# Output projection applied to keys' values before the attention product, with reordered gate, division and row-factor steps

## The reference

```python
def _L0_xattn_ref(x, mask, k_cache, v_cache, wq, wk, wv, wo):      # k_cache = v_cache = ctx
    q, k_new, v_new = x @ wq.T, x @ wk.T, x @ wv.T
    k = concatenate([k_cache, k_new], axis=1); v = concatenate([v_cache, v_new], axis=1)
    attn = softmax(q @ k.T / 16)                                    # 64 queries x 128 keys
    return (attn @ v) @ wo.T
x = x + tanh(g_xattn[0]) * _L0_xattn_ref(_layernorm(x), mask, ctx, ctx, wq, wk, wv, wo)
x = x + tanh(g_ffn[0])   * _L0_ffn_ref(_layernorm(x), w1, w3, w2)       # gated, ternary weights, hidden 682
x = x + tanh(g_xattn[1]) * _L1_xattn_ref(64, 64, 256, w, u, _layernorm(x), ctx)   # recurrence (WKV)
x = x + tanh(g_ffn[1])   * _L1_ffn_ref(_layernorm(x), ...)              # shared expert + top 2 of 8 experts
```

## Time and profile before

| | |
|---|---|
| median of 3 runs | 781.95 us (781.42 to 788.72) |
| profiled execution | 784.78 us, span of the core 783.1 us |
| busy in the span | TensorE 728.9 us, VectorE 519.7, ScalarE 353.2, GpSimd 336.2 |
| turn 0 / turn 1 / one of turns 2 to 7 / the rest | 76.2 / 72.7 / 87.4 / 109.9 us |

### The profile page before, as it was taken

The page is one execution under the profiler, slowest core; times in us unless marked ns, Lnnn a source line. Parts: engine busy times, 40 slices in busy tenths (PEclk is TensorE's granted clock), DMA queues, the critical chain, the costliest instruction groups (busy, mean ns, idle before and its releaser), DMA issues. The chain is left out here.

```text
span 783.1 us, 13120 instructions
## 1 busy us (share of the span) xinstructions
PE 728.9 (93%) x4636; PEld 624.8 (80%) x4636; DVE 519.7 (66%) x926; ACT 353.2 (45%) x676; POOL 336.2 (43%) x345
## 2 busy tenths in 40 slices
PE   6978897799999999999999999999999999897996
PEld 6876696689887888789877888789877888786785
DVE  2766467773877478773877488764877478798432
ACT  3436513564356424654356434654365434623231
POOL 2024221381545435371545345362546345275254
PEclk8999999999999999999999999999999999999899
DMA  9170002010032001220032002120022010021111
GB/s 249 64 207 9 1 1 54 28 56 28 28 82 65 32 28 53 68 64 17 27 80 68 27 27 80 42 67 13 27 80 68 27 38 29 12 58 41 55 60 49
DMA packets 36212, 41.25 MB, mean 53 GB/s; under 512 B 3198, under 2 KB 27476, under 8 KB 36180
## 3 DMA queue, kind: packets, MB, share of 16 engines
q1 hardware_dynamic: 36180, 40.83, 17.9%
HBM read 36.49 MB, written 4.33 MB: 52 GB/s over the span
## 5 line engine op out<-in xcount | busy, mean ns | idle before, releaser
L1133 POOL TENSOR_TENSOR hid_l<-act_sb,hid_h 128x512 fp32r<-128x512 f32 x120 | 162.3, 1353 | 207.9 <-ACT hid_h L938 207.6
L1381 DVE SCALAR_TENSOR_TENSOR act_sb<-act_sb,gate_ps 128x512 f32<-128x512 f32 (+1 forms) x128 | 86.8, 678 | 112.2 <-ACT act_sb L920 112.0
L1142 POOL TENSOR_TENSOR act_sb<-act_sb,late 128x512 f32<-128x512 f32 x64 | 94.2, 1472 | 73.2 <-DVE act_sb L1383 70.0
L938 ACT ACTIVATE hid_h<-act_sb 128x512 fp32r<-128x512 f32 (+1 forms) x128 | 80.4, 628 | 98.1 <-POOL act_sb L1142 62.5
L482 PE MATMUL sums<-down_h,hid_h 128*128 128x256 f32 x320 | 92.3, 288 | 5.0 <-POOL hid_l L1133 5.0
L482 PE MATMUL sums<-down_h,hid_l 128*128 128x256 f32 x320 | 90.5, 283 | 0.0
L482 PE MATMUL sums<-down_l,hid_h 128*128 128x256 f32 x320 | 90.5, 283 | 0.0
L920 ACT ACTIVATE act_sb<-gate_ps 128x512 f32<-128x512 f32 x80 | 47.3, 591 | 84.0 <-PE up_ps L482 81.1
L1383 DVE TENSOR_TENSOR act_sb<-act_sb,up_ps 128x512 f32<-128x512 f32 x120 | 82.4, 687 | 4.1
L482 PEld LDWEIGHTS sums<-down_h,hid_h 128*128 128x128 f32 x320 | 61.1, 191 | 9.5 <-issue 7.1
L482 PE MATMUL gate_ps<-zm_h,gate_h 128*128 128x512 f32 x140 | 60.9, 435 | 8.1 <-DVE act_sb L1383 8.1
(11 more groups left out here) (197 smaller groups left out, 1689.8 us busy)
## 6 DMA issues: line engine op xcount, KB each, us to landing
late<-combine_rows SPq DMA_DIRECT2D x64, 256.0 KB, 3.1
ctx_tok<-in_ctx SPq DMA_DIRECT2D x8, 512.0 KB, 5.2
vals<-in_ctx SPq DMA_DIRECT2D x16, 256.0 KB, 5.7
out_x<-late SPq DMA_DIRECT2D x8, 512.0 KB, 3.1
xa<-in_x SPq DMA_DIRECT2D x7, 512.0 KB, 3.5
wk<-in_L_ffn_w SPq DMA_DIRECT2D x2, 682.0 KB
late<-in_L_ffn_w_down SPq DMA_DIRECT2D x1, 1024.0 KB, 7.3
wk<-in_L_ffn_w_gate SPq DMA_DIRECT2D x2, 512.0 KB, 4.8
```

The costliest lines, as they stand in the source:

```text
L938: nc.scalar.activation(hid_h[0:n, pos], act_sb[0:n, pos], ACT.Copy).then_inc(hid_h_set, 1)
L1133: nc.gpsimd.tensor_tensor(hid_l[:, pos], act_sb[:, pos], hid_h[:, pos].bitcast(F32), ALU.subtract).then_inc(hid_l_set, 1)
L1142: nc.gpsimd.tensor_tensor(act_sb[:, pos], act_sb[:, pos], comb_sb[:, pos], ALU.mult).then_inc(weighted, 1)
L1381: nc.vector.scalar_tensor_tensor(mine, mine, 1.0, gate_ps[pos][0:hidden_rows(chunk)], ALU.add, ALU.mult).then_inc(gated_one, 1)
```

## The change

Own value rows and context rows are multiplied by `wo` before the attention product. For the own rows that is done once for all, in turn 0: `turn_wv` and `fuse_wv_wo` replace the value weights by their product with `wo` (it stands in PSUM, and is split from there). For the context rows `context_out` multiplies the transposed context (already in `keys`) by `wo` in each turn, in two halves of the array (64 columns of weights each), and ScalarE copies the result into `vals`. `attend` then gives the projected rows directly, with weights of 64 columns from `probsT` and 256 moving columns from `vals`. `project`, the two copies to `qo` and the two context DMAs go; the load of `wo` moves ahead of the first context load. Around it: on VectorE `scan_values(1)` and both pieces of `divide(0)` move ahead of `row_max`, and `m_gate(6)` moves behind the second statistics; on ScalarE `normalise(A, 2)` moves ahead of `m_chunk(7)`; on GpSimd `row_factors(A, 2)` moves ahead of `m_weigh(6)`. The core of the diff:

```diff
 TRANSIT:  ... ("A","v0"), ("A","v1"), +("A","u0"), +("A","u1"), ("A","scores"), ("A","pT"), -("A","oT0"), -("A","oT1"), ("A","wo0") ...
@@ sync
+                sp.dma_start(wo[:], ...)                 # at the end of attention_weights, before ctx_row
-                    sp.dma_start(vals[S:P, :, 0], ctx_seqs[t.i, 0]).then_inc(ctx_val_in, 16)
-                    sp.dma_start(vals[0:S, :, 1], ctx_seqs[t.i, 1]).then_inc(ctx_val_in, 16)
@@ tensor
+            def turn_wv():
+                pe.wait_ge(qkv_in[2], 16)
+                for m in range(KH):
+                    for k in range(KH):
+                        last = nc.tensor.transpose(gate_ps[0][:, m * D + k * P:m * D + (k + 1) * P], raw_wv[:, k, m * P:(m + 1) * P], ident[:])
+                last.then_inc(fuse_turned, 1)
+            def fuse_wv_wo():
+                pe.wait_ge(fuse_kept, 1)
+                pe.wait_ge(wo_in, 16)
+                for k in range(KH):
+                    for m in range(KH):
+                        last = nc.tensor.matmul(up_ps[0][:, k * D:(k + 1) * D], wv_turned[:, m, k * P:(k + 1) * P], wo[:, m],
+                                                start=m == 0, stop=m == KH - 1)
+                last.then_inc(fuse_done, 1)
+            def context_out(t):
+                wait_taken(pe, t, "A", "ctxT0", "ctxT1", claims=("A", "u0"))
+                for pair in range(2):
+                    bank, full = claim(t, "A", f"u{pair}")
+                    for r in range(2):
+                        for k in range(KH):
+                            for q in range(2):
+                                last = nc.tensor.matmul(bank[(1 - q) * S:(2 - q) * S, r * D:(r + 1) * D], keys[:, k, 2 * pair + r, 1 + q],
+                                                        wo[:, k], start=k == 0, stop=k == KH - 1)
+                    last.then_inc(full, 1)
             def attend(t):
-                (16 products: weights vals[:, r, q, h * P:(h + 1) * P], moving probsT[:, cols], 64 columns)
-            def project(t): ... (8 products: weights qo, moving wo[:, k], 256 columns)
+                wait_taken(pe, t, "A", "v0", "v1", "u0", "u1", "pT", claims=("A", "wo0"))
+                        for q in range(2):
+                            tile = 2 * pair + r
+                            cols = slice((2 * tile + q) * S, (2 * tile + q + 1) * S)
+                            last = nc.tensor.matmul(bank[q * S:(q + 1) * S, r * D:(r + 1) * D], probsT[:, cols], vals[:, tile, q],
+                                                    start=True, stop=True)
@@ tensor, turn
                 if first:
                     keep_clock(12)
+                    turn_wv()
                 context_T(t)
 ...
-                    keep_clock(10)
+                    fuse_wv_wo()
+                    keep_clock(4)
                 z_T(t, "A", "z0T", za_row, 1)
 ...
                 values(t)
+                context_out(t)
                 m_down(3)
                 scores(t)
 ...
                 attend(t)
                 m_up(6)
-                if first:
-                    keep_clock(3)
-                project(t)
                 m_up(7)
@@ tensor, second:  context_T, keys_T, +context_out, scores, keep_clock(10), probs_T, keep_clock(3), attend, -keep_clock(3), -project
@@ scalar
-            def attend(t): ... (2 copies 128x512 to qo)
+            def keep_wv(): ... (wait fuse_turned, 1 copy 128x512)
+            def context_out(t): ... (per pair: 2 copies of 64x512 from the bank into vals)
@@ scalar, turn
-                    for name in ("wq", "wk", "wv"): high(name)
+                    high("wq"), high("wk"), keep_wv()
 ...
                 normalise(t, "A", 1, xa, za_row, rstd_a, shift_a)
+                if first:
+                    high("wv")
 ...
                 values(t)
+                context_out(t)
                 if first:
                     act.wait_ge(tern_in, 64)   # then the absolute sums, L981
 ...
                 m_chunk(6)
+                normalise(t, "A", 2, xa, za_row, rstd_a, shift_a)
                 m_chunk(7)
-                normalise(t, "A", 2, xa, za_row, rstd_a, shift_a)
@@ gpsimd, turn
                 m_low(5)
+                row_factors(t, "A", 2, ...)
                 m_weigh(6)
                 m_low(6)
-                row_factors(t, "A", 2, ...)
@@ vector, turn
                     add_to_values(t, 0)
+                    scan_values(t, 1)
+                    divide(t, 0, 0)
+                    divide(t, 0, 1)
                 row_max(t)
                 m_gate(5)
                 row_scale(t)
 ...
-                    scan_values(t, 1)
-                    divide(t, 0, 0)
-                m_gate(6)
-                if w:
-                    divide(t, 0, 1)
                     quotient(t, 0)
                 add_attention(t)
                 wait_taken(dve, t, "A", "wo0", "wo1")
                 statistics(t, "A", 2, xa, bn_a, mv_a)
+                m_gate(6)
```

More of the change, by code:

```diff
@@ L37 @@
 SECOND = [("A", "z0T0"), ("A", "z0T1"), ("A", "q0"), ("A", "q1"), ("A", "k0"), ("A", "k1"), ("A", "v0"), ("A", "v1"),
-          ("A", "ctxT0"), ("A", "ctxT1"), ("W", "z2T0"), ("W", "z2T1")] + TRANSIT[TRANSIT.index(("A", "scores")):]
+          ("A", "ctxT0"), ("A", "ctxT1"), ("W", "z2T0"), ("W", "z2T1"), ("A", "u0"), ("A", "u1")] + TRANSIT[TRANSIT.index(("A", "scores")):]
 CHUNKS = [("M", c) for c in range(10)] + [("A", c) for c in range(6)]
@@ L248, in build @@
         tail_in = sem("tail_in")
[L250 removed]
+        x_in, ctx_row_in, out_done = sem("x_in"), sem("ctx_row_in"), sem("out_done")
         t_full = [sem(f"t_full{n}") for n in range(2)]
@@ L361, in build @@
                            qkv_l[:, n].rearrange("p k e -> p (k e)"))
-        loaded = {"wq": (qkv_in[0], 16), "wk": (qkv_in[1], 16), "wv": (qkv_in[2], 16),
+        raw_wv = raw_qkv[:, 2 * KH * D:].rearrange("p (k e) -> p k e", k=KH)
+        wv_turned = x2[:, KH:2 * KH]
+        parts["wv"] = (up_ps[0][:],) + parts["wv"][1:]
+        loaded = {"wq": (qkv_in[0], 16), "wk": (qkv_in[1], 16), "wv": (fuse_done, 1),
                   "gate": (gate_in, 32 * KH), "up": (up_in, 32 * KH), "down": (down_in, 32)}
@@ L372, in attention_weights @@
                 for n, w in enumerate((wqT, wkT, wvT)):
-                    sp.dma_start(parts[f"w{'qkv'[n]}"][0].rearrange("p (k e) -> p k e", k=KH),
+                    sp.dma_start(raw_qkv[:, n * KH * D:(n + 1) * KH * D].rearrange("p (k e) -> p k e", k=KH),
                                  w.rearrange("(k p) e -> p k e", p=P)).then_inc(qkv_in[n], 16)
+                sp.dma_start(wo[:], woT.rearrange("(k p) e -> p k e", p=P)).then_inc(wo_in, 16)
             def other_weights():
@@ L571, in project @@
                     for r in range(2):
-                        for k in range(KH):
-                            last = nc.tensor.matmul(bank[:, r * D:(r + 1) * D], qo[:, k, (2 * pair + r) * P:(2 * pair + r + 1) * P],
-                                                    wo[:, k], start=k == 0, stop=k == KH - 1)
+                        for q in range(2):
[3 more added lines that the diff above has]
+                                                    start=True, stop=True)
                     last.then_inc(full, 1)
@@ L889, in probs_T, with keep_wv, context_out @@
                 nc.scalar.activation(probsT, bank[:], ACT.Copy).then_inc(free_of("A", "pT"), 1)
-            def attend(t):
-                for h in range(KH):
-                    bank = wait_full(act, t, "A", f"oT{h}")
-                    nc.scalar.activation(qo[:, h], bank[:], ACT.Copy).then_inc(free_of("A", f"oT{h}"), 1)
+            def keep_wv():
+                act.wait_ge(fuse_turned, 1)
+                nc.scalar.activation(wv_turned, gate_ps[0][:].rearrange("p (m e) -> p m e", m=KH), ACT.Copy).then_inc(fuse_kept, 1)
+            def context_out(t):
+                for pair in range(2):
+                    bank = wait_full(act, t, "A", f"u{pair}")
+                    for q in range(2):
+                        half = slice((1 - q) * S, (2 - q) * S)
+                        last = nc.scalar.activation(vals[half, 2 * pair:2 * pair + 2, q],
+                                                    bank[half].rearrange("p (r d) -> p r d", r=2), ACT.Copy)
+                    last.then_inc(free_of("A", f"u{pair}"), 1)
             def key_weights(t):
@@ L958, in turn @@
                 if first:
-                    for name in ("wq", "wk", "wv"):
-                        high(name)
+                    high("wq")
+                    high("wk")
+                    keep_wv()
                 m_chunk(0)
@@ L991, in turn @@
                 probs_T(t)
-                attend(t)
                 if first:
```

5 lines of the change are left out of this document (2 added, 3 removed), and 4 rows, old and new, of the table TRANSIT.

## The result

The changed kernel takes **772.17 us** (median of 4 launches, 768.89 to 775.26) against 781.81 us for the kernel before on the same chip: a ratio of 0.985, 95% interval 0.981 to 0.990, so 1.5% faster. The forecast was 779.0 us, 0.4% faster, with "within 1%" as the likeliest outcome. The time lies in the range, but the likeliest outcome was the wrong one. A second series gave 773.87 against 784.15 us (0.986, 0.983 to 0.988).

A forecast was written before the change was run, and what follows sets the result against it. Full turns were taken as bound by TensorE's work and few gaps, turns 0 and 1 by waits through other engines. Full turns -6.6, turn 0 +5.6, turn 1 -2.0 gave -3.0 us: 779.0 us, range 771 to 791.

The forecast's parts named there:

- the start of turn 0: Turn 0 before its chain: `wo` landing ahead of the context and added fused work cost +1.5 us.
- the fused product against the dummies: Turn 0 on TensorE: `fuse_wv_wo` and `keep_clock(4)` replace twelve dummies' time, +0.35 us taken.
- `context_out` ahead of the sums: Turn 0: its products and copies delay ScalarE's absolute sums and VectorE's work up to the add, +3.8 us.
- The clock at z1T after the longer wait: Turn 0: TensorE's lower clock lasts longer after more idling, +0.3 us taken, 0 to 3 possible.
- The full turns: Turns 2 to 7: each -1.1 us, bounds -1.8 and +0.1; six together -6.6 us.
- Products: TensorE in each full turn: `context_out` 3.8 plus new `attend` 1.95 minus 6.76 removed, -1.0 us.
- where the gap was: TensorE's idle 0.48 us ahead of z1T in each full turn, claimed to go: -0.5 us.
- The wait ahead of m_down(6): Each full turn: TensorE waits for low_hidden(6), queued behind the normalisation, +0.4 us, bounds 0 and 1.2.
- the first rival: Full turns: no wait for chunk 6, products at their lower bound, -9.0 us in all, 773 us; chance 0.18.
- The second rival: Full turns: normalisation ahead of high_hidden(6) makes m_down(6) wait, up to 2.4 us, +9.0 in all, 791 us; chance 0.12.
- Turn 1: Turn 1's chain through `attend` and `project` shortens by -2.0 us, bounds -2.5 and -1.
- The rivals by array halves: TensorE: halves don't run side by side, 816 us, chance 0.05; or their weight loads aren't hidden, 802 us, chance 0.02.

The follow-up runs named there:

- value loads late: Kernel before, with turn 0's two loads of context rows into `vals` issued behind the load of `wo`: 781.08 us, ratio 0.999.
- `wo` first: Kernel before, with the load of `wo` moved ahead of the first context load, the two `vals` loads still behind it: 784.66 us, ratio 0.999.
- more dummies: Kernel before, with 20 dummy products instead of 12 ahead of the first context transposes, and 20 instead of 30 ahead of z1T in turns 0 and 1: 782.86 us.
- early sums, wo late: Changed kernel with turn 0's absolute sums and ternary work moved earlier, and `wo` loaded behind the first context load: 763.80 us, ratio 0.974.
- The early sums: Changed kernel with turn 0's absolute sums ahead of the query copies and `context_out`, ternary scales and two weights ahead of `row_max`: 765.26 us, ratio 0.974.
- the new order alone: Kernel before with only the reorders on VectorE, ScalarE and GpSimd, `attend` and `project` unchanged: 792.98 us, ratio 1.011.
- after again: The changed kernel, unaltered, measured once more beside the others on the same chip: 773.87 us, ratio 0.986.
- the halves one behind the other: Changed kernel with `context_out`'s loop over the array halves outermost, so each bank does one half's products first: 781.85 us, ratio 0.996.

## Why the prediction was wrong

**The step that failed** is the start of turn 0: "+1.5", from `wo` ahead of the context (+1.15) and the fused product against the dummies (+0.35). It measured -3.96 us; of the some 12 us that separate the forecast from the profiled launch, this is the largest single step (the six full turns together are 3.8). Ahead of the context I had priced the load that comes and not the two that go: I had costed those by turn 3, where the DMA engines are busy 0.17 of the time, "no wait there is for them: nothing". In turn 0 they stand right behind the load that TensorE waits for. The runs put in its place: the two loads -2.93 us (value loads late), `wo` ahead of the context +1.18 (10.04 against 8.86; +0.42 in the kernel before with `wo` first), and the clock -2.21 (6.52 us from context to queries instead of 8.73, as with more dummies). Each of these is a difference of two single launches, and with `wo` ahead the context lands anywhere from 9.33 to 10.14 us in the traces of the changed kernel and its variants. With `wo` right behind the context it landed at 10.19 (early sums, wo late), so the +1.18 is not shown to come from its place ahead. From the start of the fused product to z0T it is 2.85 us, and with ten dummies at the full clock 2.85 as well, since z0T then waits 0.46 us for ScalarE: 0 instead of +0.35. I had the two rows for the clock side by side, 1.97 against 1.09 us for like transposes, and used them for z1T only.

The Trainium skill ("DMA: Bandwidth & Descriptors", Queues, rings and completion order) says that one copy is split over up to 16 engines, that each serves its ring in order, and that loads need not complete in the order of issue. The trace agrees: the first of the two loads into `vals`, issued 0.5 us behind the context load, landed 1.2 us ahead of it (10.6 against 11.8 us in the kernel before). That the target of the later load decides, the runs alone show.

**The rest of turn 0** went as worked out. `context_out` ahead of the sums: +3.51 for +3.8. The early sums, which stand ahead of it and of the copies before it, win 8 us; how much of that is `context_out` no run separates. Another 0.2 us is gained between the sums and the ternary scales. The clock at z1T after the longer wait: +0.5 for +0.3. Sum -0.17 instead of +5.6; of the difference, 5.5 us are the start.

**The full turns**: -1.74 instead of -1.1 us, just short of the bound of -1.8. Products -1.28 (3.60 + 1.88 - 6.76) for -1.0: 3.60 us lie even under the 3.65 that I called the least. The 228 ns in it came from busy time, which runs past the next product's start; from start to start `project` took 3.27 / 16 = 204 ns for each instruction. From the start of m_down(6) to that of z1T, where the gap was, 1.43 us instead of 2.06: -0.63 for -0.5. Together that is 0.2 us more than the turn gained; the rest of the turn gives it back in small pieces. The wait ahead of m_down(6) 0 for +0.4: it was a chain with 0.26 us to spare, of which the row factors had 0.34 us less to their normalisation than the row of before gave (1.63 for 1.97). This is the first rival, "the full turns close up entirely", which I had at 0.18; with its own turn 0 of +4.3 it gave 773 us. Here it came true in the full turns, and turn 0 was better still; that the median lies next to those 773 us is luck. So is its place in the range: the bounds of the three terms end at 781.95 - 9.3 = 772.7 us, and for the 771 of the range no sum is given. The second rival's mechanism is real, as the new order alone shows (1.39 us of wait), and lay 0.26 us away.

**Turn 1**: -2.76 for -2.0 in the profiled launch. `attend` began 3.3 us later in the turn, not 3.8, and the adds of 1.65 us (108.03 on) still overlap its end. But this gain is not there in every launch. From turn 1's first transposes to turn 2's first product it is 71.98 us before, 69.23 in the profiled launch, and 72.37 in the traced launch of "after again", the same kernel. `context_out` and `scores` of turn 1, in the one and in the other:

```profile
97.18 3.03 PE L561 MATMUL transit<-wo,keys 128*64 128x256 f32 x26
...
100.69 1.97 PE L571 MATMUL transit<-keys,zqo 128*64 128x128 f32 x32
```

```profile
97.44 5.36 PE L561 MATMUL transit<-wo,keys 128*64 128x256 f32 x32
102.64 1.97 PE L571 MATMUL transit<-keys,zqo 128*64 128x128 f32 x32
```

`context_out` takes 3.51 us in the one and 5.20 in the other, where the granted clock is 0.50 from 98 to 100 us and 0.57 once more from 142 to 146. The waits ahead of it are alike (1.87 and 0.89 us, 1.85 and 0.89), so why the clock held in one launch and fell in the other stays open. The forecast had no term for it.

**The rivals by array halves** did not come. The Trainium skill ("TensorE: Matmul & The Clock Gate", Part 3, The mechanism) says in its list that weight loads overlap running products only in other rows of the array (its text also lets loads into a background buffer overlap), and that products run strictly in order. The measurement decides against both items of the list here: 137 ns of loading under products that start 112 ns apart on average, all on the same rows, and, as read from the counts, in the kernel with the halves one behind the other nine instructions under way in 0.9 us, where one half at a time has room for four or five at 228 ns each.

## What to carry to other kernels

A load that goes is to be priced at each place where it is issued, above all in the first microseconds, where all transfers run at once and a wait of TensorE costs a second time through its clock. Shorter work and a new order are one change when each fills the wait that the other opens: cost the chain as it stands after both, and keep to the engine whose queue decides (here VectorE), before moving the steps behind it. Work that only start-up needs deserves its own order: moving the absolute sums ahead was worth 8.6 us, more than the fewer products of all six full turns (6 x 1.28).

## What was not expected of the hardware

- Two loads of 256 KB into `vals` held the 16 DMA engines at 196 GB/s, busy share 1.14, where the same stretch moved 400 GB/s without them. Into another buffer the rate fell as well (272 GB/s), yet the load ahead of them landed at 10.22 us instead of 13.12.
- Products on two halves of the array, issued in blocks of eight, take 4.63 us instead of 3.60: read from the counts, they overlap only from the middle of a block on.
- 3.89 us without products cost 2.5 us more afterwards: the granted clock was 0.50 for the next 5 us (1.2 GHz).
- The same kernel ran turn 1's `context_out` in 3.51 us in one launch and in 5.20 in another, behind like waits: the granted clock stayed at 1.00 (2.4 GHz) in the first and fell to 0.50 in the second.
